# A graph layer with a routed feed-forward on one core: twelve fp32 aggregation products split into rounded parts, and row transposes placed behind the second relation

## The reference

```python
h   = t5_norm(layernorm(x)) * ln_weight
agg = h @ W_root + bias
for r in range(2):                      # relations
    w   = (edge_type == r)
    msg = h[src] @ W_rel[r] * w[:, None]            # 286 columns
    agg += segment_sum(msg, dst) / max(count(w, dst), 1)
x   = x + layernorm(x) + elu(agg) @ wo              # 286 -> 1024
z   = layernorm(x)
x   = x + z-through(2 shared experts, top 2 of 8 routed experts)
```

## Time and profile before

| | |
|---|---|
| median of three runs | 329.88 us (329.28 to 330.02) |
| the profiled execution's own time | 329.98 us |
| its span, first to last instruction | 328.0 us |
| granted TensorE clock, mean | 1.000 |
| PE busy | 318.2 us |
| DVE busy | 241.8 us |
| ACT busy | 189.7 us |
| POOL busy | 77.7 us |

### The profile page before, as it was taken

The page is one execution under the profiler, slowest core; times in us unless marked ns, Lnnn a source line. Parts: engine busy times, 40 slices in busy tenths (PEclk is TensorE's granted clock), DMA queues, the critical chain, the costliest instruction groups (busy, mean ns, idle before and its releaser), DMA issues.

```text
span 328.0 us, 6153 instructions
## 1 busy us (share of the span) xinstructions
PE 318.2 (97%) x1994; PEld 274.6 (84%) x1994; DVE 241.8 (74%) x469; ACT 189.7 (58%) x316; POOL 77.7 (24%) x94
## 2 busy tenths in 40 slices
PE   7999999999999999999999999999999999999996
PEld 2889897788789888888999888888988887878885
DVE  2999999976748456874665779977877758582885
ACT  2896999994121324442156889778878776660000
POOL 6741090001010110120213334322334310003810
PEclk9999999999999999999999999999999999999999
DMA  7970014000001126489052684989998981124995
GB/s 248 354 194 2 2 26 151 0 3 17 0 19 47 64 85 206 160 269 362 11 187 66 231 280 158 346 271 302 356 336 306 336 348 68 74 118 136 330 369 184
DMA packets 27011, 57.60 MB, mean 176 GB/s; under 512 B 2733, under 2 KB 16537, under 8 KB 26980
## 3 DMA queue, kind: packets, MB, share of 16 engines
q1 hardware_dynamic: 20452, 33.89, 30.8%
q0 software_dynamic: 3888, 14.16, 12.8%
q10 hardware_dynamic: 2640, 9.17, 7.1%
HBM read 66.25 MB, written 14.03 MB: 245 GB/s over the span
## 4 chain that ended last, share of the span: by engine, by line
PE 65%; ACT 10%; DVE 8%; DMA 7%; issue 5%; DVEq 2%; SPq 1%; ACTq 0%
PE ps L1535 41%; PE ps L1824 8%; PE ps L1659 6%; DMA y_acc<-in_x 4%; PE ps L1813 4%; DMA raw<-in_L_ffn_W 3%; ACT arena_r L772 2%; DVEq L1138 2%; PE ps L1545 2%; DVE work L1122 2%; DVE big L1135 1%; ACT sw_raw L837 1%; PE ps L1694 1%; DVE arena_r L1417 1%; ACT xt L753 1%
## 5 line engine op out<-in xcount | busy, mean ns | idle before, releaser
L1535 PE MATMUL ps<-arena_r 128*128 128x512 f32 (+1 forms) x264 | 67.9, 402 | 0.4 <-DVE arena_r L1412 0.3
L1535 PE MATMUL ps<-xt,arena_r 128*128 128x314 f32 (+3 forms) x324 | 60.3, 337 | 0.0
L1535 PE MATMUL ps<-arena_r,xt 128*128 128x286 f32 (+1 forms) x360 | 59.1, 305 | 0.4 <-DVE arena_r L549 0.3
L1535 PEld LDWEIGHTS ps<-arena_r 128*128 128x128 f32 (+1 forms) x264 | 47.8, 188 | 11.5 <-DVE arena_r L1412 0.7
L669 POOL DMA_INDIRECT big<-xrow,tok_i x17 | 35.4, 2085 | 88.9 <-PE ps L1813 70.1
L1535 PEld LDWEIGHTS ps<-xt,arena_r 128*128 128x128 f32 (+1 forms) x324 | 51.2, 187 | 5.5 <-issue 0.2
L1535 PEld LDWEIGHTS ps<-arena_r,xt 128*128 128x128 f32 (+1 forms) x360 | 49.2, 187 | 1.6 <-DVE arena_r L549 0.6
L1417 DVE TENSOR_TENSOR arena_r<-raw,arena_r 128x2048 fp32r<-128x2048 f32 x17 | 38.9, 2286 | 2.5 <-ACT arena_r L999 2.3
L1824 PE MATMUL ps<-big,tile 128*128 x160 | 37.5, 380 | 0.2 <-issue 0.2
L999 ACT ACTIVATE arena_r<-raw 128x2048 fp32r x17 | 32.3, 1903 | 2.9 <-DMA raw<-in_L_ffn_W 2.2
L1824 PEld LDWEIGHTS ps<-big,tile 128*128 128x128 f32 x160 | 29.1, 190 | 3.7 <-issue 0.4
(11 more groups left out here) (240 smaller groups left out, 467.0 us busy)
## 6 DMA issues: line engine op xcount, KB each, us to landing
big<-in_L_ffn_W SPq DMA_DIRECT2D x19, 1024.0 KB, 7.5
raw<-in_L_ffn_W SPq DMA_DIRECT2D x19, 1024.0 KB, 10.8
yrow<-work ACTq DMA_DIRECT2D x17, 512.0 KB, 4.8
raw<-in_L_gnn_W_rel SPq DMA_DIRECT2D x2, 1144.0 KB, 10.8
y_acc<-in_x SPq DMA_DIRECT2D x4, 512.0 KB, 8.2
xrow<-work SPq DMA_DIRECT2D x4, 512.0 KB, 2.9
raw<-in_L_ffn_sW SPq DMA_DIRECT2D x2, 1024.0 KB, 6.0
sw_raw<-in_L_ffn_sW SPq DMA_DIRECT2D x2, 1024.0 KB, 11.9
```

What stands on the lines that cost most here:

```text
L1535: ins = pe.matmul(out_ap, a, b, start=start and k == 0, stop=stop and k == n - 1)
```

## The change

In relation 0 of destination tiles 2, 3 and 4, the source tiles 0 to 3 are multiplied by `hilo` instead of `pe.matmul`; source tile 4 (113 rows) stays float32. That is 12 float32 products out and 36 rounded ones in. For this, ACT and DVE split relation 0 of `h_rel` of the four source tiles once (two pairs, `h_split_hi` and the loop over `h_pairs`, 128x576 each), and relation 0 of `a_t` once for each of the three destination tiles (`a_split_hi`, `a_split_lo`, 128x512 each) into one buffer that is used over again. The products of relation 0 are 288 columns wide instead of 287 in all tiles. `rows_t` of steps 2 and 3 stands behind `aggregate(s, 1)` instead of ahead of it, and DVE's `split_rows_lo` of rows 0 and 1 stands behind the statistics of the next tile.

```diff
@@ agg_views @@
-            return bank[:, 0, 0:F], [[(0, bank[:, 1, 0:F + 1])],
-                                     [(0, bank[:, 1, F + 1:F + 1 + half]), (half, bank[:, 0, F:2 * F + 1 - half])]]
+            return bank[:, 0, 0:F], [[(0, bank[:, 1, 0:HF])],
+                                     [(0, bank[:, 1, HF:HF + half]), (half, bank[:, 0, F:2 * F + 1 - half])]]
@@ ACT @@
+            def h_split_hi():
+
+                act.wait_ge(s_h, T)
+                act.wait_ge(s_hs, T)
+                act.wait_ge(s_ones, T)
+                for s, pair in h_pairs:
+                    act.activation(h_hl[0][:, s:s + 2], pair, ACT.Copy).then_inc(s_ahi, 1)
+
+            def a_split_hi(t):
+
+                cols = slice(t * P, t * P + rows[t])
+                act.activation(a_hl[0][:, :, 0:rows[t]], a_t[:, 0:NSP, 0, cols], ACT.Copy).then_inc(s_ahi, 1)
+
+            h_split_hi()
+            act.wait_ge(s_at, 1)
+            a_split_hi(2)
...
+                if s in (2, 3):
+                    act.wait_ge(s_alo, len(h_pairs) + s - 1)
+                    a_split_hi(s + 1)
@@ DVE @@
+            dve.wait_ge(s_ahi, len(h_pairs))
+            for s, pair in h_pairs:
+                dve.tensor_tensor(h_hl[1][:, s:s + 2], pair, h_hl[0][:, s:s + 2].bitcast(F32),
+                                  ALU.subtract).then_inc(s_alo, 1)
+
+            def a_split_lo(t):
+
+                cols = slice(t * P, t * P + rows[t])
+                dve.wait_ge(s_ahi, len(h_pairs) + t - 1)
+                dve.tensor_tensor(a_hl[1][:, :, 0:rows[t]], a_t[:, 0:NSP, 0, cols],
+                                  a_hl[0][:, :, 0:rows[t]].bitcast(F32), ALU.subtract).then_inc(s_alo, 1)
+
...
+                if 1 <= s < T - 1:
+                    a_split_lo(s + 1)
                 t = s - 2
-                if 0 <= t and s != T:
+                if t == 2 or t == T - 1:
                     split_rows_lo(t, T + t)
...
                     stats(t, T + t, s_x2, t + 1)
+                    if 1 <= t <= 2:
+                        split_rows_lo(t - 1, T + t - 1)
@@ PE @@
-                        ins = pe.matmul(o, a_t[0:rows[s], s, r, cols], h_rel[s][0:rows[s], r, at:at + o.shape[1]],
-                                        start=start and s == tiles[0], stop=stop and s == tiles[-1])
+                        first, last = start and s == tiles[0], stop and s == tiles[-1]
+                        if r == 0 and t >= 2 and s < NSP:
+                            ins = hilo(o, [((a_hl[0][:, s, 0:rows[t]], a_hl[1][:, s, 0:rows[t]]),
+                                            (h_hl[0][:, s], h_hl[1][:, s]))], start=first, stop=last)
+                        else:
+                            ins = pe.matmul(o, a_t[0:rows[s], s, r, cols], h_rel[s][0:rows[s], r, at:at + o.shape[1]],
+                                            start=first, stop=last)
...
+                if s >= 2:
+                    pe.wait_ge(s_alo, len(h_pairs) + s - 1)
                 aggregate(s, 0, slot0 + slot1)
...
+                aggregate(s, 1, slot0 + slot1, part=slice(1 if s == 1 else 0, 2)).then_inc(s_agg, 1)
                 if s >= 2:
                     rows_t(x3, s_x3, s - 2, T + s - 2)
-                aggregate(s, 1, slot0 + slot1, part=slice(1 if s == 1 else 0, 2)).then_inc(s_agg, 1)
...
+            pe.wait_ge(s_alo, len(h_pairs) + T - 2)
```

More of the change, by code:

```diff
@@ L164, in program @@
         h_rel = [raw[:, h_at[t]:h_at[t] + R * HF].rearrange("p (r f) -> p r f", r=R) for t in range(T)]
+        NSP = T - 1
+        h_pairs = [(s, raw[:, h_at[s]:h_at[s] + 2 * R * HF].rearrange("p (s r f) -> p s r f", s=2, r=R)[:, :, 0])
+                   for s in range(0, NSP, 2)]
+        h_hl = [cut(rel_at + i * NSP * HF, NSP * HF).rearrange("p (s f) -> p s f", s=NSP) for i in range(2)]
+        a_at = rel_at + 2 * NSP * HF
+        a_hl = [cut(a_at + i * NSP * P, NSP * P).rearrange("p (s d) -> p s d", s=NSP) for i in range(2)]
+        assert NSP % 2 == 0 and a_at + 2 * NSP * P <= wo_at
         work = sb("work", [P, 2 * D])
@@ L336, in program @@
         s_agg = sem("s_agg")
+        s_ahi = sem("s_ahi")
+        s_alo = sem("s_alo")
         s_m = sem("s_m")
```

## The result

The changed kernel takes 327.48 us (median of seven, 326.75 to 327.79), the kernel before beside it 329.27 us (median of seven, 327.86 to 330.02): a ratio of 0.9947 with a 95% interval of 0.9927 to 0.9967. That is faster, by 1.8 us. I had forecast 328.9 us and a range of 328.3 to 329.8, so the sign was right and the size too small.

What follows compares the result with a forecast made beforehand. PE was taken to bound the stage: twelve source tiles at 0.082 us gave 0.98, less 0.02 for wider float32 products, so -0.96 us; 329.98 became 329.0 profiled and 328.9 us median, range 328.3 to 329.8.

Steps and rivals of the forecast that it cites:

- The price of the products: PE, relation 0 of tiles 2 to 4: three rounded products at 0.134 us replace a 0.484 us float32 one, saving 0.082 us.
- the root row: Trace row of PE's rounded `root` products, 286 columns wide: 24 in 3.19 us, 0.133 each, the basis for the 0.134 us price.
- The covers: New splits on ACT and DVE hide behind PE; thinnest at the first tile, a 1.42 us pair with 0.35 us to spare.
- The moved transposes: PE's row transposes behind relation 1 cost 0; `s_agg` comes 0.87 us sooner, but nobody waits for the earlier elu chain.
- the first paragraph on the bound: PE, busy 38.90 of 38.90 us from 88.1 to 127.0, bounds the stage; there is no wait to remove.
- The sum: Whole kernel: -0.96 us on PE takes a profiled 329.98 us to 329.0, and the median to 328.9.
- More: Rival, chance 0.05: rounded products in relation 0 cost only 0.119 us each, saving 1.50 us, for 328.4 us.
- Weight loads show: Rival, chance 0.04: twelve more PE weight loads of 0.187 us are not hidden, costing 2.24 us, for 331.2 us.
- DVE late at the first tile: Rival, chance 0.03: DVE's pair over `h_rel` takes over 2.76 us, undoing the gain; at 3.4 us the kernel takes 330.5.
- a part only: Rival, chance 0.18: products cost as at 314 columns, or thin covers lose half the gain: -0.48, 329.4 us.
- No effect: Rival, chance 0.02: a later transfer keeps its own time and swallows the gain, leaving 329.9 us.

Runs made afterwards that it cites:

- move_only: Kernel before with the row transposes of steps 2 and 3 and DVE's remainders moved as in the change, float32 products kept: 328.85 us against 328.94, ratio 1.0005.

## Why the prediction was right or wrong

**The price of the products** was right. 0.134 us was forecast and 0.133 measured, with relation 0 at 2.08 us against a forecast of 2.09. The three tiles gave 0.34, 0.33 and 0.34 us, 1.01 in all, for the -0.96 of the sum. The gap that the Trainium skill ("TensorE: Matmul & The Clock Gate", "Back-to-back issue gap") gives for an isolated product, 122.5 ns, would have made 1.40; the runs measure 0.133 us and side with the root row.

**The covers** of the changed order were right where they were put to the test: 1.43 us and 0.36 us of idle on DVE at the first tile, no wait of PE for the splits, and the same short waits behind the last tile.

**The moved transposes** and the first paragraph on the bound are a step that failed. The prediction said that "a microsecond taken off PE between 91 and 127 us is a microsecond off the end, unless a helper becomes late" and that "the move itself costs 0", with nobody waiting for the earlier elu chain. The first held at the new order only: at the old one 1.06 us off PE gave 0.15 us of span, not because a helper became late but because PE came to the transposes before ACT's rows. By itself the move gives nothing (move_only), but without it the products give nothing either: PE's step of 12.2 us would have been below the loop of 12.57 us that goes through the transposes, and the later start of that loop behind the split takes the rest. I had priced the changed order piece by piece and found every cover sufficient, which it is. I looked at the old one for the first rows only, where ACT is ahead of PE by some tenths, and not for the second, where 109.84 stands against 109.89. So the text gave the whole saving to the products, where it takes both edits. A small part is in PE's own rows too: the second set of transposes takes 0.87 us where it took 0.95, so 0.08 us of the 1.09.

**The sum** is the step that missed the time: "329.98 - 0.96 = 329.0", and from it 328.9, where 327.48 was measured, 1.42 us less. Three terms make this up, and the saving is the smallest of them. The stage gave 1.09 us instead of 0.96, which is 0.13.

The base was too high. Three executions had a median of 329.88 us, seven have 329.27, which is 0.61. The profiled one of these three had a span of 328.0, 1.1 us above before's median span, because a load landed late in it; I read that piece as one that "starts sooner too", and it is one that comes and goes.

The rest, 0.68 us, fits a term that the prediction put at nothing without a reason, a change of the time outside the span: it stayed at 329.0 less 327.0, "some 2 us". In the five series 0.2 to 0.8 us of it went away with the change of PE's program (before's median is 1.99, 2.53, 2.55, 2.18 and 2.01, 1.71 to 1.86 in the changed kernel and its variants). For the first series this is not shown, since the record has no spans for six of before's seven executions there, and why PE's program moves this time stays open. The saving within the span came near the sum although the argument gave no worth to the edit without which it would have been nothing; that much of the agreement is luck.

**The rivals.** None of them was this. "More" had the right side but the wrong mechanism, a cheaper product. "Weight loads show", "DVE late at the first tile" and "a part only" have no trace in the rows of the changed kernel. "No effect" named the late DMA piece, but as something that would swallow the gain.

## What to carry to other kernels

Where one engine is busy for the whole of a stage, look for the loop through the other engines that returns to it once a step, and add up its length: here it was 12.57 us against a PE step of 12.49, so that savings on PE inside the loop counted for next to nothing in the median before the order was changed. The cover has to be read at every step and not only at the first: here it was 0.23 us at one and 0.05 at the next. The test is cheap: take a microsecond off the busy engine (or add one) and see what the span does. And take a span and what lies outside it from several executions before a single profile is made the base of a sum whose result is as small as their scatter.

## What was not expected of the hardware

The time outside the span went with the make-up of PE's program, by a mechanism that stays open. Three products of two columns each, with the span at 327.3 against 327.0 beside it, took the median outside from 2.18 to 1.75 us and its tail from 2.91 to 1.80. And a 1 MB weight load issued 254.4 us into the span was needed 9.6 us later and came 11.3 us later in one execution, in time in another of the same kernel, at a cost of about 1.1 us of span; with five products of two columns added behind the last one it came 11.6 us later in one execution.
